# Expert pages of 64 rows in expert order, two to a block, with the first expert matrix streamed through the tokens

## The reference, cut to what matters

```
NUM_EXPERTS = 160; TOP_K = 8; HIDDEN = 256; INTER = 128
# xf = layer norm of x;  s = sigmoid(xf @ router_w.T), the 8 best experts e(k) of each token
# out = x + shared(xf) + 2.5 * sum_k s_k / (sum_k s_k) * w_down[e(k)] @ silu(w_gate[e(k)] @ xf)
# w_gate[e]: 128 x 256    w_down[e]: 256 x 128
```

## Time and profile before

| | us |
|---|---|
| median of 3 runs, without profiler | 1448.95 (1445.54 to 1453.1) |
| span of the profiled execution | 1580.3 |
| of it: phase 1, to about 530 | 530 |
| phase 2, 530 to about 1036 | 506 |
| from there to the first expert transpose at 1054 | 18 |
| expert blocks, 1054 to 1520 | 466 |
| the last scatters and the sums, 1520 to 1580 | 60 |
| mean granted TensorE clock | 0.948 |

### The profile page before, as it was taken

How to read it: one execution, slowest core, us unless ns; L and a number is a source line. 1 busy time by engine, 2 the same in 40 slices (tenths; PEclk the granted TensorE clock), 3 DMA queues, 4 the chain that set the end, 5 groups by cost and what they waited for, 6 DMA issues and landing times. The chain is left out here.

```text
span 1580.3 us, 32555 instructions
## 1 busy us (share of the span) xinstructions
PE 1369.1 (87%) x10653; PEld 1008.8 (64%) x10653; DVE 996.6 (63%) x2910; ACT 618.7 (39%) x1909; POOL 615.5 (39%) x797
## 2 busy tenths in 40 slices
PE   7999999999987989999998998677787887878846
PEld 4666676666754666666666666466676776767645
DVE  3766666666653578867887787546665655544447
ACT  3544545444443566655665565221111111133100
POOL 1101111011101146555655555545556565555630
PEclk9999999999996899999999999889999999998978
DMA  8534244243400011111111111278878777776758
GB/s 257 191 98 142 92 142 138 95 141 100 134 1 28 14 53 53 51 63 63 50 54 64 63 36 40 70 235 266 248 232 245 233 236 250 239 218 204 227 195 351
DMA packets 153404, 221.57 MB, mean 140 GB/s; under 512 B 23789, under 2 KB 111116, under 8 KB 151320
## 3 DMA queue, kind: packets, MB, share of 16 engines
q1 hardware_dynamic: 53912, 97.83, 19.5%
q10 hardware_dynamic: 79456, 86.96, 17.6%
q0 software_dynamic: 19872, 34.71, 6.1%
HBM read 161.16 MB, written 99.61 MB: 165 GB/s over the span
## 5 line engine op out<-in xcount | busy, mean ns | idle before, releaser
L898 POOL DMA_INDIRECT y_d<-y,xg x286 | 278.6, 974 | 200.5 <-DVE y L895 126.7
L890 PE MATMUL bank<-pTC,ex 128*128 128x256 f32 x572 | 193.6, 423 | 73.2 <-ACT ex L884 41.0
L872 DVE COPY ex<-bank 128x256 f32<-128x256 f32 x286 | 120.4, 421 | 173.2 <-PE bank L868 101.9
L884 ACT ACTIVATE ex<-bank 128x128 f32<-128x128 f32 x286 | 77.6, 277 | 381.3 <-PE bank L880 222.0
L880 PEld LDWEIGHTS bank<-ex,pTC 128*128 128x128 f32 x1144 | 184.2, 207 | 51.2 <-issue 34.8
L880 PE MATMUL bank<-ex,pTC 128*128 128x128 f32 x1144 | 190.9, 293 | 17.4 <-issue 16.9
L890 PEld LDWEIGHTS bank<-pTC,ex 128*128 128x128 f32 x572 | 93.2, 205 | 91.0 <-ACT ex L884 48.9
L707 POOL DMA_INDIRECT xs_d<-xw,slot_id x128 | 131.0, 1023 | 34.6 <-issue 30.5
L895 DVE COPY y<-bank 128x256 f32<-128x256 f32 x286 | 120.5, 421 | 30.3 <-PE bank L890 18.1
L406 ACT ACTIVATE ex<-bank,nmC 128x256 f32<-128x256 f32 x256 | 119.5, 488 | 8.6 <-DVE nmC L400 8.1
L868 PE MATMUL bank<-ident,xg 128*128 128x128 f32 x572 | 116.0, 287 | 3.9 <-DMA xg<-xs_d 3.9
(11 more groups left out here) (308 smaller groups left out, 2919.5 us busy)
## 6 DMA issues: line engine op xcount, KB each, us to landing
pTC<-in_wexp SPq DMA_DIRECT2D x286, 256.0 KB
xs_d<-zeros ACTq DMA_DIRECT2D x16, 2448.0 KB, 9.7
xg<-xs_d ACTq DMA_DIRECT2D x143, 272.0 KB
cT<-in_ctx SPq DMA_DIRECT2D x32, 512.0 KB, 3.6
xg<-y_d SPq DMA_DIRECT2D x6, 1024.0 KB, 12.4
y_d<-y,xg POOLq DMA_INDIRECT x286
ex<-y_d SPq DMA_DIRECT2D x3, 1024.0 KB, 15.5
xf_d<-xw SPq DMA_DIRECT2D x16, 128.0 KB, 2.7
```

The costliest lines, as they stand in the source:

```text
L872: T.done("dve", dve.tensor_copy(xgT[z][:, :, :], bk[:, 0:2 * P].rearrange("p (c n) -> p c n", c=2)))
L884: U.done("act", act.activation(h[z][:, :], bk[:, 0:P], ACT.Silu))
L890: D.done("pe", pe.matmul(bk[:, 0:DIM], h[z][:, :], w[z][:, DIM:2 * DIM], start=True, stop=True))
L898: pool.indirect_dma_start(out=y_d, out_offset=bass.IndirectOffsetOnAxis(ap=who, axis=0), in_=y[:, n, :], in_offset=None, bounds_check=last ...
```

## The change

Pages have 64 rows, at most 416 of them, and are worked two at a time: 208 blocks of 128 rows, of which the upper and the lower half can belong to different experts.

- The page table: a tile can take up to two new pages per expert, so `need` becomes the sum of two comparisons; the expert's number is no longer written into the rows. Instead `count_pages(j)` counts on DVE, for each tile, from the scan which expert each new page went to (2 or 3 operations with a sum each).
- `order_pages` at the end of phase 2 sorts the 416 pages by expert with DVE comparisons and 8 PE matmuls, and writes two rows of numbers: the expert to load and the page to read. Sorted pages are laid on a grid of 16 slots x 26 turns, a slot holds 26 pages that follow one another, and a page whose expert is that of the turn before gets a number out of range: its weight DMA is skipped and the weights stay. Pages without an expert come last.
- Loads: SP reads two numbers and issues up to two weight DMAs of 256 KB per block, into 16 buffers; ACT reads two page numbers and issues two DMAs of 68 KB per block, 12 blocks ahead, 32 deep.
- The block: `up` holds the tokens' transposed halves stationary (64 columns each) and streams w_gate; its result has tokens on partitions, halves in partitions 0 to 63 and 64 to 127. Silu follows, then a transpose on PE with a DVE copy (`flip`, new), then `down` with two halves of 64 stationary columns. Lags are 2 (up), 4 (flip), 6 (down); `turn` has 2 PSUM banks in place of 4.
- The parts of the shared expert have other due times. The zero fill in phase 1 shrinks with the table.

```diff
-BLOCKS = -(-((TOKENS * TOPK + EXPERTS * (P - 1)) // P) // 4) * 4
+PAGE, SLOTS = 64, 16
+TURNS = -(-((PAIRS + EXPERTS * (PAGE - 1)) // PAGE) // SLOTS)
+PAGES = SLOTS * TURNS
+BLOCKS = PAGES // 2
...
-            link(dve.tensor_tensor(need[:, :], after, room[:, :], ALU.is_gt))
+            dve.tensor_copy(ends[z][:, 0:1], ends[1 - z][:, EXPERTS:EXPERTS + 1])
+            link(dve.tensor_tensor(gap, after, room[:, :], ALU.subtract))
+            link(dve.tensor_scalar(more[:, :], gap, 0.0, None, ALU.is_gt))
+            link(dve.scalar_tensor_tensor(out=need[:, :], in0=gap, scalar=float(PAGE), in1=more[:, :], op0=ALU.is_gt, op1=ALU.add))
...
-            link(dve.tensor_scalar(whole[:, :], tops[:, j, :], 1.0, None, ALU.subtract))
-            dve.tensor_scalar(slot_id[z][:, :], whole[:, :], (1 << PAGE_BITS) - 1, None, ALU.bitwise_and)
-            E.wait(dve, "xw", j)
-            R.done(j, "dve", dve.tensor_scalar(xw[z][...], whole[:, :], PAGE_BITS, None, ALU.logical_shift_right), "ids")
+            R.done(j, "dve", dve.tensor_scalar(slot_id[z][:, :], tops[:, j, :], 1.0, None, ALU.subtract), "ids")
...
+        def count_pages(j):
+            for n, c in enumerate(unsure):
+                last = dve.scalar_tensor_tensor(out=..., in0=ends[j % 2][:, 1:], scalar=page[:, c:c + 1], in1=..., op0=ALU.is_le, op1=ALU.mult, accum_out=counts[:, c, j:j + 1])
+        def order_pages():
+            link(dve.tensor_reduce(keys[:, 0, :], counts[:, :, :], AX.X, ALU.add))
+            dve.scalar_tensor_tensor(out=keys[:, 1, :], ...).then_inc(s_sort, 1)
+            for c in range(CHUNKS):
+                last = pe.matmul(bank[7][:, c * P:(c + 1) * P], bc(keys[:, 0, c:c + 1], 1, P), ident[:, :], start=True, stop=True)
+            link(dve.scalar_tensor_tensor(out=row, in0=bank[7][:, 0:PAGES], ...))
+            for c in range(CHUNKS):
+                last = dve.scalar_tensor_tensor(out=junk[c % 2], in0=row, scalar=keys[:, 1, c:c + 1], ..., op0=ALU.is_lt, accum_out=ranks[:, c:c + 1])
+                ...  dve.tensor_scalar(onehot[k], numbers, ranks[:, k:k + 1], None, ALU.is_equal)
+            for c in range(CHUNKS):
+                last = pe.matmul(bank[7][0:1, 0:PAGES], keys[:, 1, c:c + 1], onehot[c], start=(c == 0), stop=(c == CHUNKS - 1))
+            # six operations of DVE on one partition write table[0] and table[1]
...
+def load_weights(nc, a, table, n, w, s_w):
+    _, which = nc.values_load_multi_w_load_instructions(table[0][0:1, 2 * n:2 * n + 2], engines=[mybir.EngineType.SP])
+    for half, e in enumerate(which):
+        sp.dma_start(w[2 * d + half], a["wexp"][bass.ds(e, 1)]..., bounds_check="skip_entire_dma").then_inc(s_w[d], 16)
...
-    UP, DOWN, AHEAD, STRIDE, WEIGHED = 2, 4, 6, 87, 12
+    UP, FLIP, DOWN, AHEAD, WEIGHED = 2, 4, 6, 12, 9
...
+            _, which = nc.values_load_multi_w_load_instructions(table[1][0:1, 2 * n:2 * n + 2], engines=[mybir.EngineType.Activation])
+            for half, q in enumerate(which):
+                act.dma_start(xg[half * PAGE:(half + 1) * PAGE, n % FETCHED, :], pages[bass.ds(q, 1)]..., bounds_check="skip_entire_dma")
...
             for c in range(2):
-                last = pe.matmul(bk[:, 0:P], w[z][:, c * P:(c + 1) * P], xgT[z][:, c, :], start=(c == 0), stop=(c == 1))
+                for half in range(2):
+                    rows = slice(half * PAGE, (half + 1) * PAGE)
+                    last = pe.matmul(bk[rows, 0:P], xgT[z][:, c, rows], w[2 * z + half][:, c * P:(c + 1) * P], start=(c == 0), stop=(c == 1))
...
+        def flip(b):
+            V.done("pe", pe.transpose(bk[:, 0:P], hidden[z], ident[:, :]))
+            V.done("dve", dve.tensor_copy(h[z][:, :], bk[:, 0:P]))
...
-            D.done("pe", pe.matmul(bk[:, 0:DIM], h[z][:, :], w[z][:, DIM:2 * DIM], start=True, stop=True))
+            for half in range(2):
+                rows = slice(half * PAGE, (half + 1) * PAGE)
+                last = pe.matmul(bk[rows, 0:DIM], h[z][:, rows], w[2 * z + half][:, DIM:2 * DIM], start=True, stop=True)
```

More of the change, by code:

```diff
@@ L122, in phase2_weights @@
     return (tern, wf, wqd, wod, wka, wkb, wva, wvb, bqd, bkd, bvd, bod, lns, lnb, wh, bh, bg, wqk, bqk, osw, osb, wout, bout,
-            wgs, wds, wr, be, tri, ones, base, pairs, half), loads
+            wgs, wds, wr, be, tri, ones, owner, page, pairs, half), loads
 class Turns:
@@ L225, in phase2 @@
         (tern, wf, wqd, wod, wka, wkb, wva, wvb, bqd, bkd, bvd, bod, lns, lnb, wh, bh, bg, wqk, bqk, osw, osb, wout, bout,
[L226 removed]
+         wgs, wds, wr, be, tri, ones, owner, page, pairs, half) = resident
         s_set, s_max = sem("s_set2"), sem("s_max")
@@ L710, in stage_f @@
                 grow(j)
-        def first_weights():
+        def count_pages(j):
+            yield 273.00
+            few, many = P * TOPK * j // PAGE, (P * TOPK * (j + 1) + EXPERTS * (PAGE - 1)) // PAGE
+            unsure = [c for c in range(CHUNKS) if P * (c + 1) > few and P * c < many]
+            for n, c in enumerate(unsure):
+                last = dve.scalar_tensor_tensor(out=(late[:, :], spot[:, 0, :])[n % 2], in0=ends[j % 2][:, 1:], scalar=page[:, c:c + 1],
+                                                in1=owner[:, :] if j < TILES - 1 else ones_e[:, :], op0=ALU.is_le, op1=ALU.mult, accum_out=counts[:, c, j:j + 1])
+                if n % 2 and c < unsure[-1]:
+                    link(last)
+            R.done(j, "dve", last, "counted")
+            R.wait(dve, "counted", j)
@@ L713, in first_weights @@
             yield 83.87
-            sp.wait_ge(s_rows[0], 16 * TOPK)
-            with nc.allow_non_contiguous_dma(reason="one word of each page"):
-                sp.dma_start(todo_row[0:1, 0:EARLY], page_words(xs_d)[0:1, 0:EARLY, :].rearrange("p q o -> p (q o)")).then_inc(s_todo, 16)
-            sp.wait_ge(s_todo, 16)
+            sp.wait_ge(s_table, 1)
+            E.wait(sp, "yo", TILES - 1)
             D.wait(sp, "pv", TILES - 1)
-            for r in range(EARLY):
-                load_weights(sp, a, todo_row, r, w[r], s_w[r])
+            for n in range(SLOTS // 2):
+                load_weights(nc, a, table, n, w, s_w)
@@ L836, in experts @@
         last_pair = pool.to_reg(PAIRS - 1)
-        doubles = xs_d.rearrange("(q g p) n -> q p g n", g=2, p=P)
+        pages = xs_d.rearrange("(q p) n -> q p n", p=PAGE)
         link = dchain.link
-        T, U, D = (Count(nc, sem, n) for n in ("turn", "up", "down"))
+        T, U, V, D = (Count(nc, sem, n) for n in ("turn", "up", "flip", "down"))
+        hidden = [xw[0][:, :, :].rearrange("p k n -> p (k n)")[:, z * P:(z + 1) * P] for z in range(DEEP)]
         sums = "ddp" * 5 + "p"
@@ L953, in experts @@
         g = [v.rearrange("p (k n) -> p k n", k=TOPK) for v in g]
-        s_row = [sem(f"s_row{z}") for z in range(RING)]
+        s_row, used = s_w, TURNS * 32
         s_sum = [sem(f"s_sum{z}") for z in range(2)]
```

208 lines of the change are left out of this document (128 added, 80 removed).

## The result

The changed kernel takes **1565.5 us** (median of 4 runs, 1565.2 to 1568.1), the kernel before 1448.9 (1445.5 to 1453.1): a ratio of **1.0799, 95% interval 1.0776 to 1.0823**, slower by 117 us. Forecast were 1411 us and a gain. The profiled execution of the changed kernel took as long as the others: span 1563.7.

The account below looks back on a forecast made before the run. No engine was full: PE and POOL's scatters waited on each other in the expert stage. Stage -60, pipeline +5, phase 2 +8, page ordering +6 gave -41 us on 1580.3, ratio 0.974, 1411 us; range 1350 to 1485.

Parts of the forecast that it names:

- The base of the sum: Expert stage before: 466 us for 286 pages, 1.63 us a page, 0.54 of it waiting; unprofiled median 0.917 of span.
- ACT's step: Expert stage, ACT's two DMA issues, number read and silu per block: at most 1.5 us, under PE's 1.70.
- PE's block: Expert stage, PE's work per 128-row block: 1.70 us with overlapping halves and four tiling changes, 354 us for 208 blocks.
- Rival D: The two 64-column halves don't overlap on PE: 2.43 us a block, 505 us of stage, 1500 us; chance 0.04.
- The residual wait of 0.25: Expert stage: 0.25 us of waiting left per block, giving 1.95 us a block, 406 us against 466.
- Phase 2: Ranking additions on DVE mostly hide under PE: 0.5 us a tile lost, +8 us, ends 0 and 27.
- The boundary: Page ordering between phase 2 and expert stage, partly covered by the last scatters: +6 us, ends 0 and 20.
- C: PE runs out of instructions in the expert stage: 2.42 us a block with waiting, 503 us, total 1500 us; chance 0.18.
- A: All waits in the expert stage go: -93 us in the profile, 1364 us; chance 0.16.
- B: DVE's additions and page order show in full, residual wait 0.40, expert stage 437 us: total 1449 us; chance 0.13.
- E: Weight loads aren't skipped, 368 instead of 173, queues at 98%: about 1470 us; chance 0.03.
- POOL's idle time: Sign that the forecast holds: POOL's idle time before the scatters is all waiting for DVE's y.

Follow-up runs that it names:

- a_two: Changed kernel with each block's rows loaded by two 64-row DMAs from fixed places, no page number read on ACT: 1566.3 us, 0.983 of the kernel before.
- a_static1: Changed kernel with each block's rows loaded by one 128-row DMA from a fixed place, no page number read on ACT: 1532.1 us, 0.962 of the kernel before.
- a_best: Changed kernel reading four blocks' page numbers at once, loading three blocks' rows before the loop, lead growing to 12: 1501.5 us, 1.036 of the kernel before.
- b_store: Kernel before with the expert stage's scatters replaced by plain DMAs of the same 128 KB from POOL, to wrong rows: 1426.8 us, 0.987.
- b_noscatter: Kernel before with the expert stage's scatters left out, POOL writing one word instead: 1392.5 us, 0.962.
- a_again: Changed kernel, unchanged, run once more on another chip: 1593.6 us, 1.007 of the kernel before there.
- b_again: Kernel before, unchanged, run once more for trace and times on one chip: 1579.9 us, span 1577.5.
- a_read8: Changed kernel reading the page numbers of four blocks at a time on ACT, eight numbers a read: 1569.1 us, 0.984 of the kernel before.

## Why the prediction was wrong, point by point

**The base of the sum: wrong, and the largest error.** The sum counted on 466 us of expert stage, "1.63 us a page", of which 0.54 was waiting, and on the 131 us between span and median as a factor of 0.917. Both came from a trace of another chip than the timed one, on which the indirect DMAs go with pauses of PE. On the quick chip the stage of the kernel before can be put together: 285 x 1.10 = 314 us without scatters, and 56 more with them (1448.5 - 1392.5), 370 us. That is POOL's cadence of 1.28 us of the earlier trace rows over 285 intervals, 365. No trace of it was had; the figure stands on these two runs, and takes the whole difference of 56 as lying between the first and the last silu. So what the new blocks had to beat was 1.30 us a page and not 1.63. "Wrong altogether would be a gap between profile and median that moves": it moved.

**ACT's step: wrong.** "at most 2 x 0.37 + 0.5 + 0.28 for the silu queued behind them = 1.5 us, still under 1.70". Measured 1.96 to 2.06. Term by term: the read was at the upper end taken, 0.50; the silu's 0.28 doesn't hold the queue and had no place in the sum; waiting instructions and the silu's issue, 0.18, were left out; and the loads were mis-sized, 0.63 each and not 0.37. The earlier trace rows is a load of 256 rows by all 128 partitions, and what the new loads share with a_two's, which have a fixed address and cost 0.62 too, is that they fill 64 partitions. The computed address isn't the reason, or not alone; why the narrower load is dearer, no run shows. So ACT's queue, not PE, set the pace: 426 us for 208 blocks where 406 were forecast. The start was missed altogether: ACT issues in order, so the rows loaded ahead stand before the first silu, 21 us more than before. a_static1 and a_best show both. The Trainium skill ("DMA: Bandwidth & Descriptors", Anatomy of one DMA), speaking of POOL's path, calls descriptor generation small, with many descriptors to be emitted before its cost shows. On ACT's queue each load held the queue for 0.49 us; whether that is descriptor generation, no run shows.

**PE's block: nearly right, by two errors that partly cancel.** Forecast 1.70 us, with the halves overlapping and four changes of tiling. With PE full it is 1.79 us, 18 us more for 208 blocks:

```profile
1250.03 0.65 PE L967 MATMUL bank<-pTC,ex 128*64 128x256 f32 x4
1250.61 0.33 PE L956 MATMUL bank<-ident,xw 128*128 128x128 f32 x1
1250.87 0.66 PE L946 MATMUL bank<-wout,ex 128*64 128x128 f32 x8
1251.46 0.44 PE L932 MATMUL bank<-ident,xg 128*128 128x128 f32 x2
1251.83 0.65 PE L967 MATMUL bank<-pTC,ex 128*64 128x256 f32 x4
```

(a_best, start to start.) Down 0.58 and up 0.59, forecast 0.59 and 0.60 with their change; flip 0.26 and turn 0.37, forecast 0.20 and 0.31. The work without changes is less than forecast: the halves overlap fully (lines at the end), so up is 4 x 0.11, down 2 x 0.215, and with flip and turn 1.20 us and not 1.34. That leaves 0.59 for the four changes, some 0.15 each rather than the 0.09 of the earlier trace rows. Rival D falls. The residual wait of 0.25 was a guess at a cause that isn't there: none is left on the quick chip. But 208 x 1.79 = 372 us is what the old stage took. Even a perfect version of this block would gain nothing there: "taken alone PE has more to do than before" was the sentence to build on.

**Phase 2: in its range, not its value.** +8 forecast (0 to 27). On the quick chip L593 of b_store, whose phase 2 is that of the kernel before, starts for the last time at 985.5, and L604 after at 1005.8: +20, or 1.2 us a tile (periods of 29.8 and 31.0) where 0.5 was taken. The additions on DVE didn't hide under PE. **The boundary:** +6 forecast (0 to 20); from there to the first row load 29.8 us (1015.3) and 45.5 (1051.3): +16. In the two profiles the first transposes stand at 1054.52 and, 1054.35, as if nothing had been added. That was chance: an undisturbed, longer phase 2 beside a disturbed, shorter one.

**The sum with measured terms**, quick chip: phase 2 and boundary +36, start of ACT +21, blocks 426 - 370 = +56, tail from the last silu +5 (59.6 us; b_noscatter 55.0): +118, where 117 were measured. This isn't an independent check, since the 370 hold the difference of two whole times; what it shows is where the 117 lie. On the chip of a_again and b_again: +32, +21, 424 - 462 = -38, +2, that is +17 between the spans (1594.2 and 1577.5).

**The rivals.** C had the right sign, and with 1500 us the nearest time to 1565, for a wrong reason: PE doesn't lack instructions. Its evidence, was a pause under POOL's indirect DMAs. Its 2.42 us a block also isn't the 2.06 measured. The sign named for it, idle time of PE marked "issue", was ambiguous: pauses carry that mark as well. A and B assume a stage that the timed chip didn't have. E falls: the weights' queue moved 28.06 MB in 1054 to 1500 us against 52.18 in the earlier trace rows, fewer than the 45 forecast. POOL's idle time was all "DVE y" (268.1 of 272.5), as forecast.

**Left open.** What in an indirect DMA, or in the places that it writes, goes with late signals of PE, and why on five chips of six. The Trainium skill ("DMA: Bandwidth & Descriptors", Terms) says that POOL's kind of DMA has its descriptors written to rings in SBUF; plain stores from the same queue hardly disturbed, so that alone isn't it. Nor does every kernel pause: a_static1, with 56 scatters in 100 us on such a chip, kept PE full between 1100 and 1300 us. It differs from a_two in one load a block in place of two; which of its effects keeps PE full wasn't tried.

## What to carry to other kernels

Before a trace is used as the base of a sum, its span is held against the timed runs; a gap of 9% means that they aren't the same execution, and every wait in the trace has to be suspected, above all one that no engine's work explains. An engine with a low busy share can be the bound by its queue: count reads, register work, waiting instructions and DMA issues by their own durations, each load at the price of its own shape, leave out what runs on the engine meanwhile, and look at what stands in line behind them. And where an engine's bare work grows, a gain that rests on waits going away needs each wait's cause shown first.

## What the runs showed of the hardware

- The same program took 1448.5 us on one chip and 1580 to 1593 on five; without the expert stage's indirect stores 1392.5 and 1429.1. Of the 37 us left between these, 35 lie ahead of the first silu (1022.0 and 1056.6), where phase 2 keeps its indirect DMAs.
- A load into 64 partitions held ACT's queue for about 0.62 us, with a computed address (0.49 and 0.14 of register work and gaps) as with a fixed one (a_two); a load into 128 partitions for 0.33 (a_static1) to 0.37. A read of two numbers took 0.50 us, a read of eight 0.55 (a_read8). A silu of 0.28 us on the engine didn't hold the queue.
- Two 64-column groups in different halves of PE overlap fully; their starts are 0.01 us apart, and the next pair follows after the 0.11 us of one (timeline, a_best). A change of form cost 0.09 us in the earlier trace rows and some 0.15 here.

```profile
1252.83 0.27 PE L946 MATMUL bank<-wqd,ex 128*64 128x128 f32 x1
1252.84 0.27 PE L946 MATMUL bank<-wod,ex 128*64 128x128 f32 x1
1252.94 0.27 PE L946 MATMUL bank<-wqd,ex 128*64 128x128 f32 x1
1253.05 0.27 PE L946 MATMUL bank<-wqd,ex 128*64 128x128 f32 x1
```

- With 32 streamed columns a matmul PE stayed at the 1.2 GHz level for the whole stage, and the stage took 1.66 us a page, about what it took at the higher level with the pauses (1.62).
